# Centring the dense chunks of a graph kernel's first pass on TensorE, with degrees fetched and weights held in PSUM

## The reference

```python
h = maximum(layernorm(x), 0)
# layer 0, attention over edges
proj  = einsum('nf,hfg->nhg', h, w_proj)
delta = proj[src] - proj[dst]
radial     = einsum('ehf,hf->eh', delta, radial_score) - scale * edge_len
tangential = einsum('ehf,hf->eh', delta, tangential_score)
# for both: softmax over the edges of a node, sum of alpha * delta per node
x = x + (h + mean_over_heads(radial_sum + tangential_sum) @ w_out)
h = maximum(layernorm(x), 0)
# three layers of masked sums over the edges (row = src, col = dst of the same list)
for l in range(3):
    mask = clip(sigmoid(mlp(h_l[row], h_l[col])) * 1.5 - 0.45, 0, 1)
    degree = segment_sum(mask, row) + 1e-6
    d = clip(degree ** -0.5, 0, 10)
    h_{l+1} = segment_sum((mask * d[row] * d[col]) * h_l[col], row)
x = x + h_0 + h_1 + h_2 + h_3
```

## Time and profile before

| | us |
|---|---|
| median of 3 runs | 3070.73 (3069.87 to 3077.95) |
| the profiled execution, device time | 3072.85 |
| its span, first to last instruction | 3071.1 |
| DVE busy | 2284.4 (74%) |
| POOL busy | 1815.3 (59%) |
| PE busy | 1554.9 (51%) |
| ACT busy | 1085.1 (35%) |
| mean granted TensorE clock | 0.726 |

### The profile page before, as it was taken

The page is one execution under the profiler, slowest core; times in us unless marked ns, Lnnn a source line. Parts: engine busy times, 40 slices in busy tenths (PEclk is TensorE's granted clock), DMA queues, the critical chain, the costliest instruction groups (busy, mean ns, idle before and its releaser), DMA issues.

```text
span 3071.1 us, 31786 instructions
## 1 busy us (share of the span) xinstructions
PE 1554.9 (51%) x8068; PEld 1146.0 (37%) x8068; DVE 2284.4 (74%) x6153; ACT 1085.1 (35%) x2192; POOL 1815.3 (59%) x1744
## 2 busy tenths in 40 slices
PE   1123334334311888426665545656566756665664
PEld 0023333233200455224554434534444534444442
DVE  6748999999967999535565536988767978766775
ACT  0014444444420444113233334544445634443221
POOL 0057766665378688767777771147770047773776
PEclk9985556555555999757777767977888977886555
DMA  0013443343320111042222211433332433333443
GB/s 7 0 55 88 117 112 101 109 113 103 90 65 9 32 41 43 28 94 61 63 64 62 49 37 47 88 86 101 98 99 64 88 90 95 102 93 91 125 119 83
DMA packets 280174, 231.29 MB, mean 75 GB/s; under 512 B 157447, under 2 KB 210239, under 8 KB 279865
## 3 DMA queue, kind: packets, MB, share of 16 engines
q1 hardware_dynamic: 226361, 189.26, 22.2%
q0 software_dynamic: 53632, 39.99, 6.2%
HBM read 156.71 MB, written 84.30 MB: 78 GB/s over the span
## 4 chain that ended last, share of the span: by engine, by line
POOL 34%; DVE 31%; issue 15%; DVEq 10%; PE 4%; DMA 2%; ACT 2%; SPq 1%; ACTq 0%; POOLq 0%
POOL big L1009 14%; POOL G L1000 12%; POOL out L1016 6%; DVE den L1279 3%; DVE den L398 2%; DVE den L396 2%; DVE big L1293 2%; DVEq L375 2%; DVEq L550 2%; DVE big L1597 2%; DVE bank L809 2%; POOL regs L1863 1%; DVEq L810 1%; DVE den L376 1%; DVE regs L523 1%
## 5 line engine op out<-in xcount | busy, mean ns | idle before, releaser
L1009 POOL DMA_INDIRECT big<-layer_rows,late x392 | 425.8, 1086 | 303.8 <-SPq L1081 184.9
L1863 POOL DMA_INDIRECT regs<-in_x,G x200 | 202.8, 1014 | 308.3 <-DVEq L1716 174.4
L1460 PE MATMUL bank<-regs,SQ 99*128 99x256 bf16 x1764 | 275.3, 319 | 90.0 <-ACT SQ L1366 82.8
L660 POOL DMA_INDIRECT x_after_layer<-big,scat_i x200 | 239.5, 1198 | 74.3 <-issue 60.6
L1872 POOL DMA_INDIRECT regs<-in_x,G x200 | 210.0, 1050 | 121.7 <-DVE G L520 63.2
L1016 POOL DMA_INDIRECT out<-G,scat_i x196 | 195.6, 998 | 106.4 <-issue 62.0
L1279 DVE SCALAR_TENSOR_TENSOR den<-steps,late,bank 128x256 f32<-128x256 f32 x588 | 245.3, 473 | 12.1 <-PE bank L1460 12.0
L1460 PEld LDWEIGHTS bank<-regs,SQ 99*128 99x128 bf16 x1764 | 189.2, 112 | 161.4 <-ACT SQ L1366 112.1
L1000 POOL DMA_INDIRECT G<-x_after_layer,own_i x196 | 201.1, 1026 | 70.8 <-issue 61.1
L1000 POOL DMA_INDIRECT G<-x_after_layer,far_i x196 | 198.2, 1011 | 65.1 <-issue 65.1
L507 PE MATMUL bank<-regs 128*128 128x196 bf16 x800 | 161.3, 356 | 88.4 <-ACT regs L494 88.4
(11 more groups left out here) (405 smaller groups left out, 5189.0 us busy)
## 6 DMA issues: line engine op xcount, KB each, us to landing
den<-in_x SPq DMA_DIRECT2D x96, 256.0 KB, 4.1
x_after_layer<-den SPq DMA_DIRECT2D x96, 256.0 KB, 2.7
regs<-x_after_layer SPq DMA_DIRECT2D x96, 256.0 KB, 3.2
out<-regs SPq DMA_DIRECT2D x96, 256.0 KB, 2.1
XC<-row_of_far_degree SPq DMA_DIRECT2D x147, 128.0 KB, 3.4
layer_rows<-TS SPq DMA_DIRECT2D x98, 128.0 KB, 1.9
regs<-sought SPq DMA_DIRECT2D x49, 196.0 KB
regs<-row_of_edge SPq DMA_DIRECT2D x75, 128.0 KB
```

The lines of the kernel that those rows point to most:

```text
L660: g.indirect_dma_start(x1_d, bass.IndirectOffsetOnAxis(ap=scat_i[0][:, u:u + 1], axis=0), big2[:, u, :], None, bounds_check=top, oob_is_er ...
L1009: ahead(g, l, REVERSED, lambda u, l=l: g.indirect_dma_start(far[:, tile_of(u // C, u % C), :], None, xt_d[l - 1], bass.IndirectOffsetOnAxi ...
L1460: ins = pe.matmul(bank[2 + 2 * b + k // 2][:, (k % 2) * 256:(k % 2) * 256 + 256], OH[b][0:RB1 + 1, k * P:(k + 1) * P], TAB[0:RB1 + 1, part ...
L1863: g.indirect_dma_start(GR[:, c % DEEP, k, 0, :], None, a["x"], bass.IndirectOffsetOnAxis(ap=own0[:, c * C + k:c * C + k + 1], axis=0), bou ...
```

## The change

**Dense chunks of the first pass.** The rows are no longer summed and centred by DVE. PE turns a chunk (`dense_turn`, four transposes into bank 2), ACT evicts it (`dense_evict`), PE multiplies it by a constant matrix (identity less 1/64 in each 64 x 64 block) back into bank 3 (`dense_centre`), and ACT's square and DVE's scale read the centred rows there. There is one buffer of each, guarded by four new semaphores. DVE finishes both chunks in their own step. ACT and PE get a new order. PE's scores move from banks 2 and 3 into the banks of the turned differences. PE starts after the second lookup table. **Weights.** `weigh` reads the head weights from unused halves of banks 6 and 7, copied there four times; it waits for an output product, and `renew` no longer does, but at the end. **Second dense pass.** The sum and the scale of a chunk lie in bank 7. **Degrees.** In the sum stages of layers 0 and 1, 19 of the 49 chunks (`BROUGHT`) aren't looked up: SP writes the table of factors to memory, POOL fetches one value per edge with four indirect DMAs a chunk, and DVE skips the four selections.

```diff
+BROUGHT = [c for c in range(1, T1 // C) if c % 5 in (0, 3)]
...
+        XT = regs[:, 10544:11056]
+        CM = regs[:, 11400:11528]
...
+        rowstat = bank[7][:, 0:4 * RW].rearrange("p (k s r) -> p k s r", k=2, r=RW)
...
         def run_third(v, tag, c):
...
+            if tag is RUN_A:
+                v.scalar_tensor_tensor(C_[0:n], centred[0:n], 0.0, bc(st[0:n, 2], F), ALU.max, ALU.mult).then_inc(signal("dn_free"), 1)
+            else:
+                v.scalar_tensor_tensor(C_[0:n], C_[0:n], 0.0, bc(run_scale(tag, c)[0:n], F), ALU.max, ALU.mult)
...
+        def dense_turn(pe, d):
+            pe.wait_ge(signal(f"da_in{d % DEPTH}"), run_need(RUN_A, d))
+            if d:
+                pe.wait_ge(signal("dn_ev"), d)
+            for q in range(4):
+                ins = pe.transpose(bank[2][:, q * P:(q + 1) * P], run_rows(RUN_A, d)[:, 2 * q:2 * q + 2, :].rearrange("p r f -> p (r f)"), ident[:, :])
+            ins.then_inc(signal("dn_tp"), 1)
+        def dense_evict(s_, d):
+            s_.wait_ge(signal("dn_tp"), d + 1)
+            if d:
+                s_.wait_ge(signal("dn_cen"), d)
+            s_.activation(XT, bank[2][:, :], ACT.Copy).then_inc(signal("dn_ev"), 1)
+        def dense_centre(pe, d):
+            pe.wait_ge(signal("dn_ev"), d + 1)
+            if d:
+                pe.wait_ge(signal("dn_free"), d)
+            for q in range(4):
+                ins = pe.matmul(bank[3][:, q * P:(q + 1) * P], XT[:, q * P:(q + 1) * P], CM, start=True, stop=True)
+            ins.then_inc(signal("dn_cen"), 1)
```

`L0_dve`, one step:

```diff
                 norm_first(v, "g", b, rows.rearrange("p c d f -> p (c d) f"))
-                if before:
-                    run_second(v, RUN_A, before)
-                run_first(v, RUN_A, d0)
+                run_second(v, RUN_A, d0)
                 norm_second(v, "g", c, b)
-                run_second(v, RUN_A, d0)
+                run_third(v, RUN_A, d0)
                 norm_third(v, "g", c, b)
...
-                run_third(v, RUN_A, d0)
                 look_dve(v, c + AHEAD)
+                if d1:
+                    run_second(v, RUN_A, d1)
                 if c:
                     scored(c - 1)
-                if before:
-                    run_third(v, RUN_A, before)
                 if d1:
-                    run_first(v, RUN_A, d1)
+                    run_third(v, RUN_A, d1)
```

`L0_act`, one step (`after` holds the chunks of step c + 1):

```diff
                 norm_square(s_, "g", c, b)
-                if before and not by_row(RUN_A, before):
-                    run_root(s_, RUN_A, before)
-                run_square(s_, RUN_A, d0)
+                run_root(s_, RUN_A, d0)
                 norm_root(s_, "g", c, b)
-                run_root(s_, RUN_A, d0)
-                if before and by_row(RUN_A, before):
-                    run_root(s_, RUN_A, before)
+                if d1:
+                    run_square(s_, RUN_A, d1)
...
+                if after[0]:
+                    dense_evict(s_, after[0])
+                if d1:
+                    run_root(s_, RUN_A, d1)
                 look_act(s_, c + AHEAD + 1)
-                if d1:
-                    run_square(s_, RUN_A, d1)
+                if after[0]:
+                    run_square(s_, RUN_A, after[0])
+                if after[1]:
+                    dense_evict(s_, after[1])
```

`L0_pe`, one step:

```diff
+                if d1:
+                    dense_centre(pe, d1)
...
+                if after[0]:
+                    dense_turn(pe, after[0])
...
                 look_pe(pe, c + AHEAD + 1)
+                if after[0]:
+                    dense_centre(pe, after[0])
+                if after[1]:
+                    dense_turn(pe, after[1])
```

`weigh`:

```diff
+                if c >= 5:
+                    v.wait_ge(signal("n_proj"), c - 4)
+                if c in (0, 1, 2 * WHELD, 2 * WHELD + 1):
...
+                    v.tensor_copy(WUP[c % 2][:, 0:n, :], BTc[:, lo:lo + n, c % 2, :])
...
-                                bc(BT[:, tiles(c), :], F), ALU.mult).then_inc(signal("m_z"), 1)
+                                bc(WUP[c % 2][:, c // 2 % WHELD, :].rearrange("p (t h) -> p t h", h=HEADS), F), ALU.mult).then_inc(signal("m_z"), 1)
```

`L1_pool`, layer 0's sum stage:

```diff
+            g.wait_ge(signal("degrees_out"), 32)
...
+            for i in range(len(BROUGHT) + 1):
+                if i < len(BROUGHT):
+                    bring_degrees(g, 0, i, top)
+                upto = max(0, BROUGHT[i] - 3) if i < len(BROUGHT) else NC1
+                for c in range(cleared, upto):
+                    g.wait_ge(signal("z_done"), c + 1)
+                    g.memset(far[:, C * c:C * c + C, :], 0.0)
```

More of the change, by code:

```diff
@@ L401, in run_square @@
             n, (X_, C_, Q_, st), (name, i) = run_parts(tag, c), run_buf(tag, c), lane(tag, c)
-            s_.wait_ge(signal(f"{name}_cen"), i + 1)
-            if by_row(tag, c):
-                for r in range(RW):
-                    s_.activation(Q_[0:n, r], X_[0:n, r], ACT.Square, bias=st[0:n, 0, r:r + 1], scale=-float(F), accum_out=st[0:n, 1, r:r + 1])
-                s_.drain()
-                ins = s_.activation(st[0:n, 2], st[0:n, 1], ACT.Sqrt, bias=eps_c[0:n, :], scale=1.0 / F ** 3)
-            else:
-                ins = s_.activation(Q_[0:n], C_[0:n], ACT.Square)
-            ins.then_inc(signal(f"{name}_sq"), 1)
+            if tag is RUN_A:
+                s_.wait_ge(signal("dn_cen"), c + 1)
+                s_.activation(Q_[0:n], centred[0:n], ACT.Square).then_inc(signal(f"{name}_sq"), 1)
+            else:
+                s_.wait_ge(signal("dense_cen"), i - NCH + 1)
+                s_.activation(Q_[0:n], C_[0:n], ACT.Square).then_inc(signal(f"{name}_sq"), 1)
         def run_root(s_, tag, c):
@@ L414, in run_root @@
             s_.wait_ge(signal(f"{name}_var"), i + 1)
-            if by_row(tag, c):
-                for r in range(RW):
-                    ins = s_.activation(C_[0:n, r], X_[0:n, r], ACT.Relu, bias=st[0:n, 1, r:r + 1], scale=st[0:n, 2, r:r + 1])
-            else:
-                ins = s_.activation(st[0:n, 2], st[0:n, 1], ACT.Sqrt, bias=eps_c[0:n, :], scale=1.0 / F)
-            ins.then_inc(signal(f"{name}_std"), 1)
+            s_.activation(st[0:n, 2], st[0:n, 1], ACT.Sqrt, bias=eps_c[0:n, :], scale=1.0 / F).then_inc(signal(f"{name}_std"), 1)
+        centred = bank[3][:, :].rearrange("p (r f) -> p r f", f=F)
+        def dense_turn(pe, d):
[17 more added lines that the diff above has]
+            ins.then_inc(signal("dn_cen"), 1)
         def run_load(sp, tag, src, c):
@@ L537, in pairs_sp @@
                 look_sp(sp, c + AHEAD + 2)
-                for d in range(2 * c - 2, 2 * c):
+                for d in range(2 * c - 3, 2 * c - 1):
                     if 0 <= d < len(RUN_A[1]) - 1:
@@ L610, in L0_sp @@
                     seek_dst_sp(sp, c // 2 + 2)
+        WHELD = 16
+        WUP = [bank[7 - k][:, 256:512].rearrange("p (c x) -> p c x", x=C * HEADS) for k in range(2)]
+        BTc = den[:, 3200:3200 + TS16 * HEADS].rearrange("p (c k x) -> p c k x", k=2, x=C * HEADS)
         LOOKED = range(FETCHED, NC1)
@@ L847, in L0_act @@
                 look_act(s_, e)
+            dense_evict(s_, 0)
+            run_square(s_, RUN_A, 0)
             for c in range(NCH):
@@ L1077, in L1_sp @@
                 if l < 2:
-                    staged(NC1, [(0, spread), (5, store)])
+                    for j in range(2):
+                        spread(LOOKUPS[l][j])
+                    sp.wait_ge(signal("r_val"), l + 1)
+                    for h in range(2):
+                        sp.dma_start(at(degree_d, 256 * h, [[512, COLS // 2], [1, 256]]), DEGR[h * (COLS // 2):(h + 1) * (COLS // 2)]).then_inc(signal("degrees_out"), 16)
+                    staged(NC1, [(0, lambda c: spread(c) if c > LOOKUPS[l][1] else None), (5, store)])
                     for b in range(2):
@@ L1208, in place @@
             v.tensor_tensor(pos_i[:, :], DCc, VAL1[:, :], ALU.add)
+            v.drain()
+            v.memset(DCc, 10.0)
             v.memset(TAB[:, 0, :], 10.0)
@@ L1550, in _ @@
             v.memset(wo[:, :], 0.0)
+            v.memset(CM, 0.0)
+            v.drain()
+            v.memset(CM[0:F, 0:F], -1.0 / F)
+            v.memset(CM[F:P, F:P], -1.0 / F)
             v.memset(SIt, NOWHERE)
@@ L1758, in _ @@
             v.drain()
+            v.tensor_tensor(CM, CM, ident[:, :], ALU.add)
             dsts = by_row_of(DSTC[:, 0:SW])
```

145 lines of the change are left out of this document (89 added, 56 removed).

## The result

The changed kernel takes 3217.0 us (median of 4 runs, 3209.4 to 3217.9) against 3072.9 for the kernel before in the same session: ratio 1.0457, interval 1.0444 to 1.0470. The forecast was 3141, its range 3065 to 3205. Slower was right; the size was not, and the time lies above the range. The profiled execution, the fastest of the four, took 3209.4 us (span 3207.5, 136.4 more than before).

| stretch, us | before | after | difference | forecast |
|---|---|---|---|---|
| start to first scoring step | 232.1 | 231.8 | -0.3 | +2 |
| scoring loop | 657.0 | 820.0 | +163.0 | +167 |
| its end to the first weighting | 98.7 | 92.0 | -6.7 | 0 |
| first weighting to last scatter | 327.5 | 324.8 | -2.7 | -34 |
| sum stage, layer 0, and hand-over | 150.8 | 158.0 | +7.2 | -26 |

A forecast was written before the change was run, and what follows sets the result against it. Before the change DVE and POOL were taken to bound the kernel in turns. 3072.85 + 167 + 2 - 34 - 26 - 29 - 10 = 3143, 2 less against the median: 3141 us, range 3065 to 3205.

The forecast's parts named there:

- Scoring loop: Dense-chunk steps grow from 13.38 to 17.1 us in 45 of 50 steps: +167 us, ends +91 and +194.
- the walk: Scoring loop: waits followed from DVE's second variance sum through ACT and PE back to DVE, 10.78 + 6.9 = 17.7 us.
- the prediction's formula: Scoring loop: step time is 11.45 + 3.11/k us, k being PE's granted clock; 17.1 at 0.55.
- the ring: Scoring loop: in-order waits among ACT, PE and DVE close from step to step and bind it, 17.1 us taken.
- Weighing loop: Weights in PSUM make POOL's scatters 0.98 us, so POOL ends sooner after DVE: -34 us, ends 0 and -37.
- the added wait for the output product before the weighting costs nothing: Weighing loop: DVE's new wait was priced at zero because those products end in the step before.
- the tail: Weighing loop: POOL's scatters left after DVE ends, forecast to take 5 us for 43.
- Sum stages: Fetching degrees for 19 of 49 chunks saves 26 us in layer 0 and 29 in layer 1; ends +19, +2, -34 each.
- DVE then needs 15.0 - 3.5 = 11.5 us for five chunks: Sum stages: two in five chunks lose DVE's degree selection of 1.74 us each.
- POOL's bound: Sum stage of layer 0: eight fetches at 1.32 us and five memsets need 12.3 us per five chunks.
- Layer stages: Two of five DVE instructions now read PSUM, relieving POOL's gathers of part of 37 us excess: -10, ends 0 and -15.
- (c): Rival: POOL bounds sum stages at 1.90 us a fetch, PSUM operands bring nothing; 3261 at worst, some 3215; chance 0.07.

The follow-up runs named there:

- e5: Changed kernel, scoring loop reordered: PE centres and turns next chunks before the lookup products, ACT evicts the second chunk after the pair's square; 2963.6 us, ratio 0.966.
- e6: Changed kernel, but PE still makes twelve products that nobody reads for each chunk whose degrees are fetched; 3195.2 us, ratio 1.038.
- e15: Changed kernel with new orders in scoring loop, weighing loop and sum stages (PE, ACT, SP), and twelve unread products kept per fetched chunk; 2862.7 us, ratio 0.931.
- e7: Changed kernel, sum stages: PE's lookup products one chunk earlier, SP's ids two chunks earlier; 3265.0 us, ratio 1.064.
- e18: Changed kernel, scoring and weighing loops reordered; in sum stages ACT's copies and SP's stores later, PE's order unchanged; 3865 us, disturbed session.
- e13: Kernel before with the fetching of degrees alone, weights and row statistics left in SBUF; 3085.5 us, ratio 1.0029.
- e12: Changed kernel without the fetching, with new orders in the scoring loop (PE, ACT) and weighing loop (PE); 3713 us, disturbed session.
- e14: Changed kernel without the fetching, with new orders in the scoring loop (PE, ACT) and weighing loop (PE); 2938.0 us, ratio 0.955.
- e3: Changed kernel with PE's output products first in a step of the weighing loop; 4036 us, disturbed session.

## Why the prediction was right about the sign and wrong about the size

**Scoring loop (+167, measured +163).** Right in the walk, and by e5 right in the cause; that the number came out within 4 us is partly luck. I took 0.55, the mean clock of the loop before, for the clock of the burst. The loop's mean is now 0.69, for which the prediction's formula gives a ring of 16.0, but the burst has 0.50 and 0.55, for which it gives 17.4. Against the walk at the lower clock (17.7) the step is 0.6 us shorter: products of 3.25 us for 3.43, turnings of 0.89 for 1.08, 0.4 in ACT's work and the hand-overs, less 0.12 for a longer centring. By the Trainium skill, page "TensorE: Matmul & The Clock Gate", section "Part 4: PE-mode transpose", the ring would be 17.7. The runs don't decide on that rule: the clock rose during the turnings (0.67 in their mean), but PE had done 5.1 us of products just before.

**Small terms.** The start cost nothing (+2 forecast). That the stretch up to the weighting would shrink I had not seen: the last dense chunks are done earlier in their step, so SP's queue is free earlier for the ids of the scan (its first transfer of them goes out 3.3 us after the loop's end instead of 11.0), for which DVE waits 13.6 us instead of 21.2; the wait in the changed kernel:

```profile
DVE regs L776 <- DMA den<-tile_nodes: 13.6, 1, 13.6
```

**Weighing loop (-34, measured -3).** The step that failed is "the added wait for the output product before the weighting costs nothing: those products end in the step before". The step that I had read, that of the earlier trace rows, ran at the higher clock. Its stretch in the kernel before, and the output products there:

```profile
1142.00:1146.00 4.00, 4.00 (x24) 2.37 (x22) 3.83 (x6) 2.96 (x6) 3.24 (x3) 1.00 0.05 17
```

```profile
1141.24 1.10 PE L951 MATMUL bank<-wo,den 64*128 64x64 f32 x8
```

Even there they end at 1142.34, 0.1 us after the weighting's start at 1142.23: the step had no margin. The output products stand last in PE's step, and at 1.2 GHz the eight turnings ahead of them take 1.92 us for 1.09; then DVE waits up to 2.6 us. In the kernel before the same products were needed only by the renewal, behind the scan and the guard. The other half was right in its cause: POOL's scatters fell to 0.98 and the tail from 41 to 13. It was 5 in the forecast, which let POOL end one chunk behind DVE; but DVE renews the last three chunks within 3 us (from 1452.5 to 1455.4), and POOL needs 5.1 for each. The Trainium skill, page "SBUF — State Buffer", section "Who interferes with whom", infers that such an instruction doesn't hold up a DMA's descriptors, only GpSimd's reads. In these traces it holds up the scatter: in the kernel before 46 of the 200 scatters overlap a weighting and 42 of them last 1.80 us or more, none of the other 154 over 1.00; in the changed kernel 65 overlap one and none of these lasts over 1.00. Whether it is the descriptors that wait or POOL's reading of the row ids (`scat_i`) from SBUF the runs don't part.

**Sum stages (-26 and -29, measured +7 and +6).** The step that failed is "DVE then needs 15.0 - 3.5 = 11.5 us for five chunks", with POOL as the only rival bound. It took DVE's work as its time. In the kernel before DVE waited for next to nothing in this stage (0.8 us), because each chunk of 3.0 us covered PE's turning back and 1.48 us of products; a chunk of 1.3 us covers neither. I priced what was removed and not what it had hidden. That PE with less to do falls from 0.98 to 0.69 made it worse by 11 to 14 us a stage (e6). POOL's price (1.30 a fetch for 1.32) was right, and 11.2 us for five chunks is what e15 reaches (109.8 us over 9.8 groups of five). It lies under the 12.3 that I took for POOL's bound, which was so too high.

**Layer stages (-10, measured -27).** Only the size was off: all 392 gathers fell from 1086 ns to 1018 in the mean (1094 in the part of the first stage that I had read the earlier trace rows), so nearly three quarters of the 37 us of excess went, not two fifths.

**The rivals.** (c), with 3215 us, is near the number by luck (half of its 120 us would give 3201, and 3215 has no sum behind it) and wrong in both mechanisms: a fetch costs 1.30 and not 1.90, and the operands in PSUM bring 27 us in the layer stages and 28 in the weighing loop's tail. The range was too narrow since each stage had ends for its own durations only, and none for a wait that appears where cover goes.

## What to carry to other kernels

When work is taken from the bounding engine, list what its time had hidden on the others, and look for each in-order queue at what stands between the last result and the next one needed: the same instructions took 3217 us and 2872 us by their order on three queues. A new order on one queue can close a ring through another: e7 alone lost 23 us a stage, with ACT's and SP's share it gained 36 to 37, and in e18 their share without PE's left DVE's wait as it was. So shift the queues of a ring together. Price a wait at PE's lower clock as well as at the one in the step you happen to read.

## What the runs showed of the hardware

PE's granted clock fell when 19 of 49 chunks lost their twelve products: 0.98 to 0.69 in the sum stage, and rose to 0.95 with products that nobody reads (e6). Fewer products were not less PE time: 99.7 us of busy PE for 100.0.

The weighting (128 x 1024, 1.21 us), with both inputs in SBUF, holds up an indirect DMA that POOL starts about when it starts; with one input in PSUM it doesn't. In the kernel before 42 of the 200 scatters last 1.80 us or more. Each of them starts between 0.08 us before and 0.27 us after the start of a weighting and ends 0.86 to 0.91 us after its end; in e13, with the weights in SBUF as well, 44 are that long. In the changed kernel the longest of the 200 takes 1.03 us.

The same kernel can meet sessions in which transfers seem to land late: the kernel before took 3474 to 3587 us, and e12 and e14, one kernel, had ratios of 1.072 and 0.955. Instructions last as long there (a gather of L1084 1010 ns in e3, 1018 in the changed kernel), and the packets take as long too (16.2% of 4024.5 us are 652, 20.6% of 3207.5 are 661); the time goes between them. What makes it so isn't shown by these traces.
